# The head of a fused AdaLN and FFN kernel: W3 loaded first, q by products that stream W3, x summed by token halves

## The reference, cut to what matters

```python
q_emb = relu(cond @ W3 + b3)                      # [64, 512]
x1    = (64 * x + x.sum(axis=1, keepdims=True)) * q_emb[:, None, :]
y     = relu(x1 @ W2 + b2)
base  = y @ W_base + b_base
share = (y @ A_s) @ B_s
gates = softmax(y @ W_router + b_router)          # top 2 of 6 experts kept
route = sum_e gate_e * ((y @ A_r[e]) @ B_r[e])
out   = x + base + share + route
```

## Time and profile before

| what | value |
|---|---|
| median of three runs | 237.88 us |
| the profiled execution, its own time | 238.09 us |
| its span in the trace | 236.2 us |
| TensorE matmuls busy | 230.7 us (98%) |
| TensorE weight loads | 188.2 us (80%) |
| VectorE | 166.7 us (71%) |
| ScalarE | 86.3 us (37%) |
| GpSimd | 49.0 us (21%) |
| instructions | 3092 |

### The profile page before, as it was taken

How to read it: one execution, slowest core, us unless ns; L and a number is a source line. 1 busy time by engine, 2 the same in 40 slices (tenths; PEclk the granted TensorE clock), 3 DMA queues, 4 the chain that set the end, 5 groups by cost and what they waited for, 6 DMA issues and landing times.

```text
span 236.2 us, 3092 instructions
## 1 busy us (share of the span) xinstructions
PE 230.7 (98%) x1008; PEld 188.2 (80%) x1008; DVE 166.7 (71%) x309; ACT 86.3 (37%) x171; POOL 49.0 (21%) x57
## 2 busy tenths in 40 slices
PE   7999899999999999999999999999999999999994
PEld 2988587878888888888888888888888888888883
DVE  0694999698979978398747969299665976055344
ACT  2266851535136240353206340263305351152330
POOL 6179342022123211022012030122110130000000
PEclk9999999999999999999999999999999999999999
DMA  7999902618043541706245451709120270104004
GB/s 198 317 218 224 277 17 40 172 56 300 8 117 89 195 163 29 182 29 221 112 87 121 175 183 18 179 14 298 57 33 0 111 244 12 22 0 178 3 0 178
DMA packets 33009, 28.80 MB, mean 122 GB/s; under 512 B 6325, under 2 KB 23413, under 8 KB 32998
## 3 DMA queue, kind: packets, MB, share of 16 engines
q1 hardware_dynamic: 31194, 28.50, 42.9%
q10 hardware_dynamic: 1804, 0.17, 0.6%
HBM read 18.89 MB, written 8.39 MB: 115 GB/s over the span
## 4 chain that ended last, share of the span: by engine, by line
PE 87%; SPq 6%; DVE 2%; DMA 2%; issue 0%; DVEq 0%
PE m_ps L743 78%; PE hT L743 9%; SPq L206 3%; DMA x_quart<-in_x_dram 2%; DVE out_nat L621 1%; SPq L228 1%; SPq L222 1%; SPq L225 1%; SPq L232 1%; DVE xT L467 0%; DVE vsum L472 0%; DVE x_sum L479 0%; SPq L229 0%; DVE y_lo L493 0%; SPq L231 0%
## 5 line engine op out<-in xcount | busy, mean ns | idle before, releaser
L304 POOL TENSOR_TENSOR x_full<-x_sum,qT 128x512 f32<-128x512 f32 x28 | 32.4, 1157 | 136.8 <-DVE x_sum L479 136.8
L348 ACT ACTIVATE y_hi<-m_ps,b_sb 128x512 fp32r<-128x512 f32 x32 | 22.0, 687 | 82.3 <-PE m_ps L743 80.3
L743 PE MATMUL m_ps<-Wb_hi,y_lo 128*128 128x512 f32 x128 | 49.9, 390 | 0.0
L743 PE MATMUL m_ps<-Wb_lo,y_hi 128*128 128x512 f32 x128 | 49.9, 390 | 0.0
L743 PE MATMUL m_ps<-Wb_hi,y_hi 128*128 128x512 f32 x128 | 49.9, 390 | 0.0
L743 PE MATMUL m_ps<-x_hi,W_hi 128*128 128x512 f32 x112 | 43.9, 392 | 0.0
L743 PE MATMUL m_ps<-x_lo,W_hi 128*128 128x512 f32 x112 | 43.7, 390 | 0.0
L743 PE MATMUL m_ps<-x_hi,W_lo 128*128 128x512 f32 x112 | 43.6, 390 | 0.0
L493 DVE TENSOR_TENSOR y_lo<-m_ps,y_hi 128x512 fp32r<-128x512 f32 x32 | 21.7, 679 | 30.2 <-ACT m_ps L350 30.2
L467 DVE STREAM_TRANSPOSE xT<-x_quart 128x512 f32<-128x512 f32 x28 | 30.4, 1087 | 3.1 <-DMA x_quart<-in_x_dram 3.1
L743 PEld LDWEIGHTS m_ps<-Wb_lo,y_hi 128*128 128x128 f32 x128 | 24.0, 188 | 5.0
(11 more groups left out here) (97 smaller groups left out, 256.4 us busy)
## 6 DMA issues: line engine op xcount, KB each, us to landing
out_dram<-out_nat SPq DMA_DIRECT2D x32, 256.0 KB, 2.2
x_quart<-in_x_dram SPq DMA_DIRECT2D x28, 256.0 KB, 4.7
x_nat<-in_x_dram SPq DMA_DIRECT2D x7, 1024.0 KB, 6.0
gatesT<-wT SPq DMA_DIRECT2D x28, 48.0 KB
x_nat<-in_x_dram SPq DMA_DIRECT2D x4, 256.0 KB, 3.6
W_f<-in_L_cond_W_dram SPq DMA_DIRECT2D x4, 256.0 KB, 7.5
Wb_f<-in_L_ffn_W_base_dram SPq DMA_DIRECT2D x1, 1024.0 KB, 9.8
W_sb<-in_L_cond_W_dram SPq DMA_DIRECT2D x1, 512.0 KB, 6.1
```

What stands on the lines that cost most here:

```text
L304: nc.gpsimd.tensor_tensor(per_batch(x1_full[:, c, :]), per_batch(x1_sum[:, c, :]), qT[:, c, bass.ds(BG * g, BG)].unsqueeze(2).to_broadcast ...
L348: nc.scalar.activation(y_hi[:, m, :], m1_ps[m][:, :], ACT.Relu, bias=b2_sb[:, m:m + 1]).then_inc(y_hi_ready, 1)
L743: mm = nc.tensor.matmul(psum, lhsT, rhs, start=start and i == 0, stop=stop and i == len(terms) - 1)
```

## The change

Five things move, all ahead of the first `h`.

1. SyncE loads W3 first, in two halves (k = 0, 1), then the x tiles.
2. q is made by two float32 products in which cond transposed (64 columns) is stationary and W3 streams, 512 columns each. The result is q with the batch on the partitions. VectorE copies it to SBUF in two copies (`q_copy`, with the features put in the order of the chunks), TensorE transposes its four chunks into one bank, and ScalarE's four `q_relu` follow. The `keep_warm` calls are 7 at the start, 1 after the turn of cond, 4 before `m1_first`.
3. `head_ps` is one tensor of four banks; a bank holds two chunks of one token half. `sum_head` works on a chunk's half of 256 tokens: eight reductions and eight additions instead of four and four. x tiles 0 and 1 are turned before q's chunks are, tiles 2 and 3 after.
4. b2 is loaded by ScalarE as its third DMA; all four A_r chunks are now issued by SyncE, where two were ScalarE's.
5. `m1_first` goes chunk by chunk to the end; before, its chunks 2 and 3 went by pairs of output tiles. ScalarE splits W2 chunks 1 to 3 and W_base earlier in its order, and GpSimd takes the rest of W_base chunks 0 and 1 ahead of Wd's.

```diff
-    WARM_LOAD, WARM_W3 = 9, 4
+    WARM_LOAD, WARM_COND, WARM_SUM = 7, 1, 4
...
+        head_ps = ctx.enter_context(nc.psum_tensor("head_ps", [P, 2, 2, 2, TG // 2], F32))
...
+        def head_x(c):
+            return head_ps[:, c % 2, :, c // 2, :]
...
@@ sync
+            for k in range(QC):
+                sp.dma_start(W3_sb[:, k, :], W3[k * P:(k + 1) * P, :]).then_inc(W3_loaded[k], 16)
             for t in range(TT):
                 sp.dma_start(x_nat[0][:, t, :], x_groups[0][:, t, :]).then_inc(head_loaded[t], 16)
-            sp.dma_start(W3_sb[:, :, :], W3.rearrange("(k p) d -> p k d", p=P)).then_inc(W3_loaded, 16)
...
-            load_A_r(sp, range(KC // 2, KC))
+            load_A_r(sp, range(KC))
             load_quarters(1, 1)
-            sp.dma_start(b2_sb[:, :], b2.rearrange("(k p) -> p k", p=P), allow_slow_non_contiguous=True).then_inc(b2_loaded, 16)
...
@@ scalar
+            act.dma_start(b2_sb[:, :], b2.rearrange("(k p) -> p k", p=P), allow_slow_non_contiguous=True).then_inc(b2_loaded, 16)
...
-            act.wait_ge(zeroed, 3)
-            load_A_r(act, range(KC // 2))
...
@@ vector
+            def q_copy(chunks):
+                dve.wait_ge(q_done, 1)
+                nc.vector.tensor_copy(q_nat[:, chunks, :],
+                                      q_ps[0:B, :].rearrange("b (f c) -> b c f", c=KC)[:, chunks]).then_inc(q_copied, 1)
...
+            q_copy(slice(0, 1))
+            q_copy(slice(1, KC))
+            for c in range(KC):
+                sum_head(c, 0, c + 1)
+            sum_head(0, 1, KC + 1)
             scale_head(0)
-            scale_head(1)
-            rest_head(0)
...
+            for c in range(1, KC):
+                sum_head(c, 1, KC + c + 1)
+                rest_head(c - 1)
+                scale_head(c)
+            rest_head(KC - 1)
...
@@ tensor
-            keep_warm(WARM_W3)
+            keep_warm(WARM_COND)
+            pe.wait_ge(condT_copied, 1)
+            for k in range(QC):
+                pe.wait_ge(W3_loaded[k], 16)
+                q = nc.tensor.matmul(q_ps[0:B, :], condT[:, k, :], W3_sb[:, k, :], start=(k == 0), stop=(k == QC - 1))
+            q.then_inc(q_done, 1)
+            turn_head(range(TT // 2))
+            for c in range(KC):
+                pe.wait_ge(q_copied, min(c + 1, 2))
+                turn = nc.tensor.transpose(qT_ps[:, c * B:(c + 1) * B], q_nat[:, c, :], ident[0:B, 0:B])
+            turn.then_inc(q_turned, 1)
+            turn_head(range(TT // 2, TT))
+            keep_warm(WARM_SUM)
```

More of the change, by code:

```diff
@@ L728, in _, with turn_head @@
             last.then_inc(condT_done, 1)
[L730 to L733, removed]
-                                               x_nat[0][:, t, :].rearrange("p (f c) -> p c f", c=KC)[:, c], ident[:, :])
-                    if t == TT - 1:
-                        turn.then_inc(head_turned, 1)
-            keep_warm(WARM_W3)
+            def turn_head(tiles):
+                for t in tiles:
+                    pe.wait_ge(head_loaded[t], 16)
+                    for c in range(KC):
+                        turn = nc.tensor.transpose(head_x(c)[:, t // 2, (t % 2) * P:(t % 2 + 1) * P],
+                                                   x_nat[0][:, t, :].rearrange("p (f c) -> p c f", c=KC)[:, c], ident[:, :])
+                        if t % 2 == 1:
+                            turn.then_inc(head_turned, 1)
+            keep_warm(WARM_COND)
[5 more added lines that the diff above has]
+            turn_head(range(TT // 2))
+            for c in range(KC):
+                pe.wait_ge(q_copied, min(c + 1, 2))
[3 more added lines that the diff above has]
+            keep_warm(WARM_SUM)
             def product(psum, terms, start, stop):
@@ L758, in m1 @@
                 mm.then_inc(m1_done, 1)
-            def q(c):
-                for k in range(QC):
-                    mm = nc.tensor.matmul(q_ps[c][:, 0:B], W3_sb[:, k, :].rearrange("p (f c) -> p c f", c=KC)[:, c],
-                                          condT[:, k, :], start=(k == 0), stop=(k == QC - 1))
-                mm.then_inc(q_done, 1)
             def m1_first():
@@ L772, in chunk @@
                                             stop=k == KC - 1 and x1 is x1_lo)
-                for k in range(KC // 2):
+                for k in range(KC - 1):
                     pe.wait_ge(x1_hi_ready, k + 1)
@@ L786, in m1_first @@
                         chunk(m, k, W2_hi, x1_lo)
-                for tiles in ((0, 1), (2, 3)):
-                    for k in range(KC // 2, KC):
-                        pe.wait_ge(x1_hi_ready, k + 1)
-                        pe.wait_ge(W2_lo_ready, k + 1)
-                        for m in tiles:
-                            chunk(m, k, W2_hi, x1_hi)
-                            chunk(m, k, W2_lo, x1_hi)
-                            pe.wait_ge(x1_lo_ready, k + 1)
-                            last = chunk(m, k, W2_hi, x1_lo)
-                            if k == KC - 1:
-                                last.then_inc(m1_done, 1)
+                k = KC - 1
+                pe.wait_ge(x1_hi_ready, k + 1)
+                pe.wait_ge(W2_lo_ready, k + 1)
+                for m in range(KC):
+                    chunk(m, k, W2_hi, x1_hi)
+                    chunk(m, k, W2_lo, x1_hi)
+                    pe.wait_ge(x1_lo_ready, k + 1)
+                    chunk(m, k, W2_hi, x1_lo).then_inc(m1_done, 1)
             def h(g, k, first):
@@ L841, in expand @@
                 nc.tensor.matmul(hT[:, :], pick[:, :], w_quads[:, :], start=True, stop=True).then_inc(gates_done, 1)
-            pe.wait_ge(W3_loaded, 16)
-            pe.wait_ge(condT_copied, 1)
-            for c in range(KC):
-                q(c)
             def step(g, par):
```

88 lines of the change are left out of this document (44 added, 44 removed).

## The result

The changed kernel takes 239.79 us (median of 4 runs, 239.36 to 239.92) against 237.87 us of the kernel before on the same chip (4 runs, 237.66 to 238.07): a ratio of 1.0081, 95% interval 1.0064 to 1.0098. It is 1.9 us slower. The forecast was 238.5, the range 237.5 to 240.4. The profiled execution took 239.92 us with a span of 238.2, 1.83 more than the one before (238.09).

What follows compares the result with a forecast made beforehand. R, when h gets its first y_lo, was taken as the later of 25.95 (x_quart's landing) and 25.8 (m1_first): +0.6 against 25.36. Median 237.88 + 0.6 = 238.5 us, range 237.5 to 240.4.

Steps and rivals of the forecast that it cites:

- rival B: TensorE's clock falls in its 3.1 us standstill before m1_first: +3.2, time 241.1, for a shorter spell 239.5; chance 12%.
- T0: Start of m1_first on TensorE, 12.66 before; forecast 14.3, bounds 13.4 and 15.0; up to 13.9 said to cost nothing.
- the lower bound that I had named: End of TensorE's q products: forecast 8.0, bounds 7.15 and 8.7; 1.9 us for the passes at the upper clock level.
- The x_quart chain: Two more A_r loads ahead of x_quart on SyncE's queue: landing 22.65 instead of 22.04, R = 25.95, +0.6.
- the engines have no more to do: The moved A_r loads' packets were there before, so DMA engines get no added work; only the queue place is new.
- a later issue widens that gap: DMA engines were 52% busy between 16 and 17 us, run dry before x_quart; issuing it later was to delay it further.
- the middle: Value taken for x_quart's delay, between 0 and 1.2 us: +0.6.
- The m1 chain at a constant clock: TensorE from m1_first to h's first y_lo: 14.3 + 11.47 gives R = 25.8, bounds 24.9 and 26.5.
- R: Moment when h gets its first y_lo, 25.36 before; forecast 25.95; all TensorE work behind it moves with it one to one.
- A: Rival: x_quart lands as before, SyncE's new issues falling into held time, q early; R 25.1 to 25.8, 238.0; chance 26%.
- C: Rival: SyncE's queue holds each new A_r load, x_quart lands 2.4 to 4.8 later, 240.3 to 242.7; chance 12%.
- D: Rival: x_quart lands before 21.6 and T0 is below 13.4; R = 24.9, time 237.4, faster; chance 8%.

Runs made afterwards that it cites:

- warm17: The changed kernel with 17 instead of 4 idle products ahead of m1_first: 239.18 us.
- after_xq: The changed kernel with group 1's second x_quart issued ahead of W_router, A_s and A_r on SyncE, and Wd's split later: 239.57 us.
- bdelay2: The kernel before with two spare reductions on VectorE ahead of the first x1, their result unused: 239.10 us.
- before_xq: The kernel before with group 1's second x_quart issued ahead of W_router, A_s and A_r on SyncE, and Wd's split later: 238.45 us.
- order: The changed kernel with chunk 0's two half sums among VectorE's first three, instead of behind the first halves of all four chunks: 238.58 us.
- warm17_ar: warm17 with A_r's first two chunks issued by ScalarE again: 238.59 us.
- bdelay5: The kernel before with five spare reductions on VectorE ahead of the first x1, their result unused: 241.02 us.
- order_b2: order with b2's load behind condT on ScalarE and eight idle products instead of four: 238.68 us.
- order_b2_xq: order_b2 with x_quart's transfers issued ahead of W_router, A_s and A_r on SyncE: 237.62 us.
- order_y8: order with eight idle products instead of four, and VectorE's first y_lo ahead of the x_quart work, the other three between its first pieces: 240.38 us.
- order_y8_b2: order_y8 with b2's load issued by ScalarE behind condT: 239.98 us.

## Why the prediction came out as it did

The time lies in the range and the sign was right. The most likely case was not the one that happened: rival B, given 12%, did, at a smaller price than stated, and the range held it only because it left room for the lower parts of the rivals. As to the mechanism, that was luck.

*T0.* Forecast 14.3, measured 14.12: right, by errors against each other. q took 1.93 us for four passes, the lower bound that I had named, and ended at 7.1 instead of 8.0. I had priced a pass like four transposes of 128 columns; it costs 0.43 us at the lower pace, so the transposes' 0.215 each was not their columns. But VectorE could not use it, for x tile 1 landed at 7.84 (5.65 after 2.19), and the sums started at 8.55. The half sums cost 0.79 to 0.80 start to start (8.55, 9.35, 10.14), as worked out; the multiplication started at 12.74, not 12.9.

*The x_quart chain.* Forecast +0.6, measured +0.07. The issues start at 15.31 instead of 14.43, the landing is the same; "the engines have no more to do" fits this, and "a later issue widens that gap" was wrong here. In warm17, with the same loads, it was +0.7. So the term is 0.1 to 0.7 by the run, and the middle was a fair value of a thing that one trace doesn't fix.

*The m1 chain at a constant clock.* Forecast R = 25.8 and, with x_quart, 238.5. after_xq's run with the clock up is the nearest to this case, though its `x_quart` is issued earlier: T0 14.02, R 25.68, 238.49. This part of the sum stands.

*Rival B.* This is the step that failed: I gave 12% to a fall of the clock in the 3.1 us pause, because "no such fall is in the trace". It happened in all 4 runs of the changed kernel and in 5 of 6 of after_xq. Its price was set too high at +2.8 (239.5 for a shorter spell was near): 12 products at 0.424 instead of 0.229 would be 2.3, the trace shows +1.6 from T0 to R, and 1.1 in the time between like runs.

The fault is in part one of sampling: the one profiled execution of before had clock 0.999, and 42 of 65 other runs of that same kernel had it at 0.985 to 0.993. Their median is 237.85, that of the 23 others 237.89. So a fall was there all along and cost nothing. I take it that it lay in the head, hidden by the 1.2 us that TensorE waited for `x_quart`, and that the change (and bdelay2, with 0.7 later T0) spent that slack and laid the fall open. That is argued, not shown: no trace of a run of before with the clock down was taken. With the 13.0 us from T0 to R of bdelay2 and before_xq (11.95 to 24.98, less its wait), R would be 25.7, 0.3 behind 25.36, and the medians don't show even that.

How the 1.9 us divide is known only roughly. By the trace 1.63 of the 1.86 us at R are the clock and 0.23 the later T0 beyond the slack. By the times the clock is less: 1.1 in after_xq, and 0.6 back in warm17, whose T0 and `x_quart` came later. The rest goes to the later T0 and to what keeps order 0.6 above its profiled run.

The Trainium skill, "TensorE: Matmul & The Clock Gate", section "What's actually happening", says that the clock follows how busy the array has been, and section "What you observe" that the moment of the rise at the start differs from run to run. The counts above (5 of 6, 42 of 65) show something near the second, that whether the clock falls differs from run to run; the moment itself no run here shows twice in one kernel. With the first, the changed head agrees: 9 of 10 runs with the 3.08 us pause lost the clock and none of 16 with idle products in it. But a TensorE row that reads 1.00 busy is no proof of activity in that sense: in before_xq it read 1.00 up to the fall.

*Rivals A, C, D.* A's mechanism for `x_quart` was true (it landed as before), but T0 then decided. C didn't happen: two more issues held SyncE for 0.67, and the first `x_quart` issue started at 15.31, not behind 17. D's condition, T0 below 13.4, wasn't met.

*Not foreseen: behind R.* I took every later piece as moving with R, one to one. In bdelay2 R is 1.03 later than before and the span only 0.3 longer (236.5 against 236.2). The three kernels with an early R show the next wait, VectorE's work for group 1. It does not touch the changed kernel, whose weight load waits there for 0.7 us as before.

Left open: where the clock was down in before's 42 runs; why order's median lies 0.6 above its profiled run; how the 0.6 between warm17 and warm17_ar comes about, since R is the same in their profiles; and whether a kernel with Wd in time and `x_quart` early is really faster than before, which wasn't run.

## What to carry to other kernels

Slack on the critical engine can hide more than waits: here the clock was down in two of three runs of the kernel before, at no cost in time, most likely behind 1.2 us of slack. Before a change that uses up such slack, look at the granted clock of all runs, not of the profiled one alone, and price the fall (here 0.7 to 1.6 us) as likely. When a stage has two chains that end together, move both or expect nothing, and look one stage further for who does the work that you put off.

## What the runs showed of the hardware

- In the old head, where sixteen q passes of 64 columns run without a gap, the clock fell with no pause (before_xq, 12.1 us), before one of 2.82 us began (bdelay5) and inside one of 0.86 (bdelay2; down in 10 of 10 runs). In the changed head it went with the pause: with one of 3.08 us the runs' mean clock was down in 9 of 10 (changed, after_xq), with 1.49 in none of 12 (order), and with seventeen idle bfloat16 products in the pause in none of 16 (warm17, warm17_ar). So the pause's length alone doesn't sort the cases. Of the 22 runs of order_b2 and order_b2_xq, with eight idle products, one lost it; order_y8 and order_y8_b2 have the same eight, kept the clock in the head of their traces and lost it at 42 us.
- A SyncE issue of A_r (768 rows of 64 bytes) took 1.7 us on average (6.72 for four) while the DMA engines' busy share was about 1.0 (8 to 14 us), and even x_quart's four took 6.43 in such a stretch (before_xq, from 6.20), against 2.14 when issued at 15.31.
- VectorE's x_sum, with two inputs in SBUF, takes 0.69 us alone, 1.18 in the changed kernel, 0.91 in warm17 and 1.78 in before_xq. Each time it ended 0.54 to 0.55 us after the GpSimd subtraction that was under way:

```profile
23.07 1.78 DVE L480 SCALAR_TENSOR_TENSOR x_sum<-xT,vsum 128x512 f32<-128x512 f32 x1
```
```profile
23.02 1.29 POOL L310 TENSOR_TENSOR Wd_lo<-Wd_f,Wd_hi 128x512 fp32r<-128x512 f32 x1 [0.95 <-ACT Wd_hi L392]
24.27 1.73 POOL L310 TENSOR_TENSOR Wb_lo<-Wb_f,Wb_hi 128x512 fp32r<-128x512 f32 x1
```

The GpSimd subtraction behind it took 1.73 instead of 1.29. The Trainium skill, "SBUF — State Buffer", section "SBUF: two separate sides", says that a VectorE instruction with two SBUF inputs and a GpSimd one that reads SBUF exclude each other for a whole instruction. These rows agree as far as they go: x_sum, started 0.05 us behind the subtraction, ends 0.54 us behind its end (24.31, 24.85), like the two others, and the time shows as length of the row, not as a wait. In before_xq this put 1.1 us on the chain that ended last, of which half counts, since TensorE alone would have reached R at 24.98.
